# Two adapter layers with Strassen-like weight products: s3 and t3 ahead of t1, an earlier half of a21, b21 copied at once, batch 0's sums on VectorE

## The reference

```python
def _L0_cond_ref(x, labeler_index, W, lora_A, lora_B_w):        # lora_A: (5, 1024, 32), lora_B_w: (1024, 32)
    base = jnp.einsum('bsi,oi->bso', x, W)
    low = jnp.einsum('bsi,bir->bsr', x, lora_A[labeler_index])
    return base + jnp.einsum('bsr,or->bso', low, lora_B_w) * (16 / 32)

def _L1_cond_ref(x, adapter_mapping, W, b, lora_As, lora_Bs):   # lora_As: (32, 1024, 16), lora_Bs: (32, 16, 1024)
    base_out = jnp.einsum('bti,oi->bto', x, W) + b
    lora_h = jnp.einsum('bti,bir->btr', x, lora_As[adapter_mapping])
    return base_out + jnp.einsum('btr,bro->bto', lora_h, lora_Bs[adapter_mapping]) * (32 / 16)

x = x + _L0_cond_ref(x, itok_B_0_2, L0_cond_W, L0_cond_lora_A, L0_cond_lora_B_w)    # x: (8, 256, 1024)
x = x + _L1_cond_ref(x, itok_B_0_23, L1_cond_W, L1_cond_b, L1_cond_lora_As, L1_cond_lora_Bs)
```

## Time and profile before

| what | value |
|---|---|
| median of 3 runs | 321.42 us (320.12 to 324.49) |
| the profiled execution | 322.18 us, of which its span is 320.4 us |
| PE busy | 304.6 us (95%) |
| DVE, ACT, POOL busy | 235.1 us (73%), 140.8 us (44%), 69.1 us (22%) |
| V made, first matmul of batch 0 | 119.21 us |
| first low-rank matmul of batch 0 | 144.60 us |

### The profile page before, as it was taken

The page is one execution under the profiler, slowest core; times in us unless marked ns, Lnnn a source line. Parts: engine busy times, 40 slices in busy tenths (PEclk is TensorE's granted clock), DMA queues, the critical chain, the costliest instruction groups (busy, mean ns, idle before and its releaser), DMA issues.

```text
span 320.4 us, 4335 instructions
## 1 busy us (share of the span) xinstructions
PE 304.6 (95%) x1397; PEld 247.8 (77%) x1397; DVE 235.1 (73%) x310; ACT 140.8 (44%) x223; POOL 69.1 (22%) x84
## 2 busy tenths in 40 slices
PE   7995998999999997789999999999999999999995
PEld 5884887788888886547878878878878878878874
DVE  2539885697999999997687687687677777776321
ACT  4554364939647715333424524425424424335110
POOL 5610000010005500061025034033043052052000
PEclk9999899999999999959999999999999999999999
DMA  6999400430003510046246255255264165103002
GB/s 197 303 356 239 54 0 2 72 61 2 0 0 53 88 25 0 1 67 164 57 77 155 57 91 138 57 85 144 57 101 138 48 101 160 25 8 123 0 33 99
DMA packets 99362, 27.55 MB, mean 86 GB/s; under 512 B 84885, under 2 KB 93077, under 8 KB 99350
## 3 DMA queue, kind: packets, MB, share of 16 engines
q1 hardware_dynamic: 99350, 27.41, 36.9%
HBM read 19.01 MB, written 8.39 MB: 86 GB/s over the span
## 4 chain that ended last, share of the span: by engine, by line
PE 67%; DVE 21%; issue 6%; ACT 3%; DMA 1%; SPq 0%; DVEq 0%
PE bank L980 65%; DVE vt_lo L617 4%; DVE xt L815 2%; PE bank L1002 2%; DVE s_lo L617 2%; DVE vt L617 2%; DVE v L617 1%; DVE t_lo L617 1%; DVE t L617 1%; DMA n<-in_L_cond_W 1%; DVE lhs_lo L617 1%; DVE v_lo L617 1%; DVE s L617 1%; DVE a_lo L617 1%; ACT a_hi L417 1%
## 5 line engine op out<-in xcount | busy, mean ns | idle before, releaser
L980 PE MATMUL bank<-vt_hi,s_hi 128*128 128x512 f32 x96 | 37.5, 390 | 0.0
L980 PE MATMUL bank<-vt_lo,s_hi 128*128 128x512 f32 x96 | 37.5, 390 | 0.0
L980 PE MATMUL bank<-vt_hi,s_lo 128*128 128x512 f32 x96 | 37.4, 389 | 0.0
L815 DVE STREAM_TRANSPOSE xt<-raw 128x512 int32<-128x512 int32 x32 | 32.2, 1081 | 0.0
L417 ACT ACTIVATE lhs_hi<-xt 128x512 fp32r<-128x512 f32 x32 | 19.8, 630 | 28.0 <-PE bank L980 17.8
L617 DVE TENSOR_TENSOR s_lo<-s_sum,s_hi 128x512 fp32r<-128x512 f32 x32 | 27.6, 886 | 2.9 <-ACT s_hi L417 2.9
L980 PE MATMUL bank<-v_hi,lhs_hi 128*128 128x512 f32 x64 | 26.0, 406 | 3.4 <-issue 3.4
L617 DVE TENSOR_TENSOR lhs_lo<-xt,lhs_hi 128x512 fp32r<-128x512 f32 x32 | 24.7, 778 | 4.4 <-ACT lhs_hi L417 4.1
L417 ACT ACTIVATE s_hi<-s_sum 128x512 fp32r<-128x512 f32 x32 | 19.9, 629 | 17.5 <-PE bank L980 9.3
L980 PE MATMUL bank<-v_lo,lhs_hi 128*128 128x512 f32 x64 | 26.8, 419 | 0.0
L980 PE MATMUL bank<-v_hi,lhs_lo 128*128 128x512 f32 x64 | 25.8, 403 | 0.0
(11 more groups left out here) (163 smaller groups left out, 754.4 us busy)
## 6 DMA issues: line engine op xcount, KB each, us to landing
raw<-in_x SPq DMA_DIRECT2D x32, 256.0 KB, 4.9
out<-y SPq DMA_DIRECT2D x32, 256.0 KB, 2.1
n<-in_L_cond_W SPq DMA_DIRECT2D x16, 256.0 KB, 5.2
a<-in_L_cond_W SPq DMA_DIRECT2D x16, 256.0 KB, 5.3
a_raw<-in_L_cond_lora_A SPq DMA_DIRECT2D x8, 128.0 KB, 2.4
a_raw<-in_L_cond_lora_As SPq DMA_DIRECT2D x8, 64.0 KB, 2.4
b_raw<-in_L_cond_lora_Bs SPq DMA_DIRECT2D x8, 64.0 KB, 2.0
b_raw<-in_L_cond_lora_B_w SPq DMA_DIRECT2D x1, 128.0 KB, 5.7
```

Source lines behind the costliest of these rows:

```text
L815: nc.vector.transpose(xt[:, n, :, :].rearrange("p e (s sb) -> p sb e s", sb=GR).bitcast(I32), rows[:, n // 2, n % 2].bitcast(I32)).then_in ...
L980: return nc.tensor.matmul(ps, lhsT, rhs, start=start, stop=stop, skip_group_check=more)
```

## The change

It moves work between places and engines and adds none but a few waits. On SP two of a21's four loads go ahead of n12's. On PE the turns of b22 and b12 stand earlier between M1's last rows of matmuls, the last b12 turn ahead of `q_step`, and the last b21 turn inside M6's second half. On DVE s3 and t3 are made first and t1 after them, `t1_t3` is split in two, and many sums and low parts of the V stage stand in another order (s1's low parts ahead of s4's, t4's low parts before M3's results are added). The two semaphore offsets S1_AT and S4_AT change places with them. ACT copies each row of b21 to `b21` right behind its high part, and PE then waits for the low part instead of the copy before it turns into that bank; ACT's `ym` copies, t1 and v11 high parts move too. Batch 0's four sums go from POOL (`sums(0)`) to DVE (`first_sum`), and in batch 0 `u_total` stands ahead of all four turns of the next x. The loop body of batches 1 to 7 has the same instructions in the same order.

```diff
@@ sync
+            for j in range(0, 2):
+                load_a(a21, 1, 0, j, a21_in[0])
             for j in range(HK):
                 load_n(n12, 1, 0, j, n12_in[j // 2])
-            for j in range(HK):
-                load_a(a21, 1, 0, j, a21_in[j // 2])
+            for j in range(2, HK):
+                load_a(a21, 1, 0, j, a21_in[1])
@@ gpsimd
-            pool.wait_ge(v_done, M3 + HK)
-            sums(0)
             pool.wait_ge(c_lo_made, 2)
@@ scalar
-            for m in range(HK):
-                act.wait_ge(v_done, M1 + m + 1)
-                bank_copy(m1, m, LOW[m], vm1_made)
-            for h in range(2):
-                act.wait_ge(t3_made, 2 * h + 2)
-                high(t3_hi, t3, PAIR[h], t_hi_made)
-                act.wait_ge(s3_made, h + 1)
-                high(s3_hi, s3, PAIR[h], vs_hi_made)
+            m1_copies(range(2))
+            s3_high(0)
+            t3_high(0)
+            m1_copies(range(2, HK))
+            s3_high(1)
+            t3_high(1)
...
                 bank_copy(b21_hi, j, TURN_BANK[j % 3], w1_hi_made)
-                act.wait_ge(w1_lo_made, HK + j + 1)
                 bank_copy(b21, j, TURN_BANK[j % 3], w1_made)
@@ vector
-            t1_t3(0)
-            t1_t3(1)
             s3_sum(0)
-            t1_t3(2)
+            t3_sum(0)
+            t3_sum(1)
+            t1_sum(0)
+            t1_sum(1)
+            s3_low(0)
             t3_low(0)
-            s3_low(0)
-            t1_t3(3)
             s3_sum(1)
+            t3_sum(2)
+            t3_sum(3)
+            s3_low(1)
             t3_low(1)
-            s3_low(1)
             for h in range(2):
+                if h == 1:
+                    t1_sum(2)
+                    t1_sum(3)
+                t2_sum(h)
                 s1_sum(h)
                 s2_sum(h)
-                t2_sum(h)
                 t2_low(h)
                 s2_low(h)
...
-            vt23(0)
-            vt23(1)
-            for h in range(2):
-                dve.wait_ge(t_hi_made, T4_AT + h + 1)
-                low(t4_lo, t4, t4_hi, PAIR[h], t_lo_made)
-            vt23(2)
             dve.wait_ge(q_done, 2)
-            turn_x(0, range(1))
-            vt23(3)
-            turn_x(0, range(1, 4))
+            for m in range(HK):
+                vt23(m)
+                turn_x(0, (m,))
             for m in range(HK):
                 vt23_low(m)
+            dve.wait_ge(xt_made, 4)
+            first_sum(0, xt[:, 2, :, :], xt[:, 3, :, :], ALU.add)
+            dve.wait_ge(s_sum_made, 1)
+            first_sum(1, s_sum[:, 0, :, :], xt[:, 0, :, :], ALU.subtract)
+            first_sum(2, xt[:, 0, :, :], xt[:, 2, :, :], ALU.subtract)
+            dve.wait_ge(s_sum_made, 2)
+            first_sum(3, xt[:, 1, :, :], s_sum[:, 1, :, :], ALU.subtract)
...
                 tt(u2_sum[:, :], BANK_B[:, :], m1_sum[:, :], ALU.add, u2_made)
+                if first:
+                    dve.wait_ge(zeroed, 4)
+                    u_total(b)
                 if not final:
                     dve.wait_ge(s_sum_made, 4 * b + 4)
                     turn_next(b + 1, range(2))
-                if first:
-                    dve.wait_ge(zeroed, 4)
-                else:
+                if not first:
                     dve.wait_ge(u_lo_made, b)
-                u_total(b)
+                    u_total(b)
@@ tensor
                 elif 2 * HK <= old < 3 * HK:
-                    pe.wait_ge(t3_made, old - 2 * HK + 1)
+                    pe.wait_ge(t1_made, old - 2 * HK + 1)
                 elif old >= 3 * HK:
-                    pe.wait_ge(w1_made, old - HK + 1)
+                    pe.wait_ge(w1_lo_made, old - 2 * HK + 1)
...
-            turn_b21(HK - 1)
-            pe.wait_ge(w1_lo_made, 2 * HK)
             for j in range(HK):
+                pe.wait_ge(w1_lo_made, HK + j + 1)
                 last = q_step(Q_BANK[0], HK + j, B21, j, False, j == HK - 1)
```

More of the change, by code:

```diff
@@ L442, in _, with m1_copies, s3_high, t3_high @@
                 bank_copy(b22, j, TURN_BANK[(HK + j) % 3], w1_made)
-            for m in range(HK):
-                act.wait_ge(v_done, M1 + m + 1)
-                bank_copy(m1, m, LOW[m], vm1_made)
-            for h in range(2):
+            def m1_copies(rows):
+                for m in rows:
+                    act.wait_ge(v_done, M1 + m + 1)
+                    bank_copy(m1, m, LOW[m], vm1_made)
+            def s3_high(h):
+                act.wait_ge(s3_made, h + 1)
+                high(s3_hi, s3, PAIR[h], vs_hi_made)
+            def t3_high(h):
                 act.wait_ge(t3_made, 2 * h + 2)
                 high(t3_hi, t3, PAIR[h], t_hi_made)
-                act.wait_ge(s3_made, h + 1)
-                high(s3_hi, s3, PAIR[h], vs_hi_made)
+            m1_copies(range(2))
[4 more added lines that the diff above has]
+            t3_high(1)
             def s2_t2_high(h):
@@ L474, in _ @@
                 high(a12_hi, a12, j, w0_hi_made)
-            for m in range(HK):
-                bank_copy(ym, m, LOW[m], vy_made)
             def q_half(h):
@@ L495, in _ @@
             copy(ct[:, 0:H], C_BANK[0][:, :], ct_made)
+            for h in range(2):
+                high(s1_hi, s1, PAIR[h], vs_hi_made)
             act.wait_ge(b0a1_done, 1)
             copy(q_part[:, 0:G1], B0A1_BANK[64:96, 0:G1], b0a1_part_made, LORA0_SCALE)
-            act.wait_ge(b0a1_all_made, 1)
-            q_half(1)
-            p_high(1)
             act.wait_ge(vs_lo_made, S2_AT + 2)
@@ L504, in _ @@
                 high(s4_hi, s4, PAIR[h], vs_hi_made)
-            for h in range(2):
-                high(s1_hi, s1, PAIR[h], vs_hi_made)
+            act.wait_ge(b0a1_all_made, 1)
+            q_half(1)
+            p_high(1)
+            for m in range(HK):
+                bank_copy(ym, m, LOW[m], vy_made)
             for h in range(2):
@@ L509, in _, with v11_high @@
                 high(a22_hi, a22, PAIR[h], w0_hi_made)
-            for m in range(HK):
+            def v11_high(m):
                 act.wait_ge(v11_made, m + 1)
@@ L514, in _ @@
                 high(t1_hi, t1, PAIR[h], t_hi_made)
+            for m in range(HK - 1):
+                v11_high(m)
             act.wait_ge(t_lo_made, T2_AT + 2)
@@ L760, in _, with b21_low @@
             tt(a1d[:, :, :], raw_a1[:, HK:KT, :], raw_a1[:, 0:HK, :], ALU.subtract, a1d_made)
-            for j in range(HK):
-                dve.wait_ge(w1_hi_made, HK + j + 1)
+            def b21_low(j):
+                dve.wait_ge(w1_made, 2 * HK + j + 1)
                 tt(b21_lo[:, j, :], TURN_BANK[j % 3][:, :], b21_hi[:, j, :].bitcast(F32), ALU.subtract, w1_lo_made)
+            b21_low(0)
+            b21_low(1)
+            t4_sum(0)
+            b21_low(2)
+            b21_low(3)
             for j in range(HK):
@@ L769, in _ @@
             b22_low(1)
+            s4_sum(0)
+            s4_sum(1)
+            p_low(0)
             dve.wait_ge(a1d_made, 1)
@@ L782, in _ @@
                                            in1=q_part[:, 0:G1], op0=ALU.mult, op1=ALU.add).then_inc(b0a1_all_made, 1)
+            s1_low(0)
+            s1_low(1)
             q_half(1)
[L784 removed]
             for h in range(2):
@@ L787, in _, with t1_low, t4_low @@
                 low(s4_lo, s4, s4_hi, PAIR[h], vs_lo_made)
+            p_low(1)
+            def t1_low(h):
+                dve.wait_ge(t_hi_made, T1_AT + h + 1)
+                low(t1_lo, t1, t1_hi, PAIR[h], t_lo_made)
+            def t4_low(h):
+                dve.wait_ge(t_hi_made, T4_AT + h + 1)
+                low(t4_lo, t4, t4_hi, PAIR[h], t_lo_made)
             def v11_sum(m):
@@ L795, in _ @@
             v11_sum(0)
+            a22_low(0)
+            a22_low(1)
             v11_sum(1)
-            s1_low(0)
             v11_sum(2)
-            s1_low(1)
+            t1_low(0)
+            t1_low(1)
             v11_sum(3)
-            for h in range(2):
-                a22_low(h)
+            t4_low(0)
+            t4_low(1)
             for m in range(HK):
                 v11_low(m)
-            for h in range(2):
-                dve.wait_ge(t_hi_made, T1_AT + h + 1)
-                low(t1_lo, t1, t1_hi, PAIR[h], t_lo_made)
             def turn_x(b, quarters):
@@ L880, in h_and_low @@
                 tt(u_st[64:64 + UB, :], u_sum[0:UB, :], u_st[0:UB, :].bitcast(F32), ALU.subtract, u_lo_made)
-            a0_low(0)
             for g in range(4):
                 a_low(0, g)
+            for h in range(2):
+                dve.wait_ge(c_hi_made, h + 1)
+                tt(c_lo[:, HK * h:HK * h + HK, :], CT_BANK[h][:, :].rearrange("p (t n) -> p t n", t=HK),
+                   c_hi[:, HK * h:HK * h + HK, :].bitcast(F32), ALU.subtract, c_lo_made)
+            a0_low(0)
             for j in range(4):
@@ L1107, in _ @@
                     by_halves(h, S2, T2, m, v_done)
+                    if h == 1 and m == 2:
+                        turn_b21(HK - 1)
                 if h == 0:
```

36 lines of the change are left out of this document (17 added, 19 removed).

## The result

The changed kernel took 310.52 us (median of 4 runs, 309.16 to 311.65) against 321.7 us (4 runs, 320.12 to 324.49): ratio 0.964, 95% interval 0.956 to 0.973. Its profiled execution took 311.65 us, with a span of 309.8. The prediction had 310.0 for the median and 308.8 for the span (310.6 - 1.8).

What follows compares the result with a forecast made beforehand. Limits in turn: DVE's low parts for M7, then PE, then DVE's backlog, met in batch 0. `low_rank` -13.2, clock +1.6, total -11.6: the profiled execution's 322.18 becomes 310.6, median 310.0; range 307.5 to 315.5.

Steps and rivals of the forecast that it cites:

- M7: In the front: M7 starts at 26.2, 3.4 us earlier, without a pause, so the clock stays full, 1.6 us more.
- b21's `q_step`: Behind M6: starts at 49.75 instead of 56.53, 6.8 us in all, of which 1.6 is the pause ahead of it.
- The margin of 0.4: Ahead of M6's second half: DVE's low parts done at 43.4, needed at 43.8, so no stall.
- DVE's backlog: From a22's low part (68.4) to the end of U's split in batch 0: 69.75 shrinks to 62.7, ending at 131.4.
- contention: In vt2's and vt3's splits: POOL's sums stretch four of eight to 1.77 from 0.68; moving the sums saves 4.4 us.
- The earlier U is what makes this the only pause: Batch 0: U leaves its bank at 122.3, so the product before `low_rank` starts at once and PE waits only at `low_rank`.
- the pause of 3.35: In batch 0 before the change: PE's idle time before 137.40, counted as lost and expected to go.
- The pause and the clock: At `low_rank` in batch 0: PE waits 2.8 us, and the low clock behind it costs 1.6, ends 0 and 3.6.
- Rival 4: Clock stays low behind batch 0's pause, into the loop: 45 us at half clock would be 331; chance 0.03.
- Rival 2: DVE does not start on a22 6.4 earlier, its backlog absorbs the front: gain about 4 to 5, 316.5; chance 0.08.
- rival 3: The splits' 1.77 came from x's load under way, not POOL's sums, and remains: +4.4, 314.2; chance 0.04.
- Rival 1: The front stays late: a miss opens a pause ahead of M7 or in M6, price 3.4 + 1.6, 315.0; chance 0.10.

Runs made afterwards that it cites:

- experiment 8: The changed kernel without the V stage's new order on DVE and ACT and without the earlier U: 314.65 us, ratio 0.978.
- experiment 1: The changed kernel with batch 0's four sums back on POOL: 314.81 us, ratio 0.980.
- experiment 2: The changed kernel with `u_total` behind two transposes again, as before the change: 309.78 us, ratio 0.967.
- experiment 9: The changed kernel with only the V stage's order as before, the earlier U kept: 316.4 us, ratio 0.984.
- experiment 5: The changed kernel with all of a21 loaded behind n12 again: 311.19 us, ratio 0.967.
- experiment 3: The kernel before with the change's front alone (load order, s3 and t3 first, PE's turns, b21's copies): 315.37 us, ratio 0.984.
- experiment 4: The kernel before with batch 0's four sums on DVE as the only change: 320.36 us, ratio 0.997.

## Why the prediction was right, and where not

**M7** was forecast at 26.2 and came at 27.14. PE was free at 26.75 instead of 26.2, mostly because M1 began at 8.04 instead of 7.31: the second turn of n11 waited 1.3 us for its load, where it had waited 0.6. The other 0.39 (the row calls 0.23 of it idle) was for t3's low part, which ended at 27.04, at a length of 1.49 instead of the 1.21 of the earlier trace rows, while POOL added the eye to a22 beside it. The prediction had left 0.15 between the two. The clock stayed at full speed behind M7, 1.6 us, as forecast.

**b21's `q_step`** came at 51.18, not 49.75, so the front gave 5.35 us and not 6.8. M7's lateness is 0.94 of the 1.43. The margin of 0.4 ahead of M6's second half is the next: s2's low part ended at 43.85 + 1.23 = 45.08, and M6's second half started at 45.13, behind a wait of 0.28 of PE's weight load. From M7 to there are 17.99 us instead of 17.6, and from there to `q_step` 6.05 instead of 5.95. The pause ahead of `q_step` is gone, as forecast.

**DVE's backlog** was the best part. Forecast 63.0 from a22's low part to the end of U's split (68.4 to 131.4), measured 62.55. The front was 1.45 late at a22 (69.85 for 68.4), and the backlog gave 0.45 of that back. Its three terms stood apart in the runs: low parts moved into earlier pauses -5.15 (experiment 8: 4.2 moved, 4.7 less in the last stretch), contention -4.4 (the eight splits 9.29 before and 4.85 now; experiment 1: 3.3 + 1.1), sums +2.5 (2.55). The worth of the move was underrated: 4.4 - 2.5 is 1.9, and experiment 1 showed 3.4. Of the 1.5 between them 1.06 is the op that writes `ac`: in the change it is done before POOL's next sums begin (127.49 against 127.93), in experiment 1 it runs into the first of them.

**"The earlier U is what makes this the only pause"** is the step that failed. Undone in the change it costs nothing (experiment 2), and without the V stage's order it only moves the wait to low_rank (experiment 9). What removed the pause of 3.35 is that DVE reaches U earlier, and for that the order of the V stage is worth 4.7 us from M7 to the split (110.0 against 105.3) and 3.7 to 4.1 of time (314.65 against 310.98 and 310.52). The order does this with U early (105.3 in the change) or late (105.3 in experiment 2), and the early U gained nothing with either order. Which part of the order does it, DVE's or ACT's, was not tried apart.

**The pause and the clock.** 2.8 us forecast, 2.25 measured. U's split ended 1.0 later than forecast, but PE also got to low_rank later, at 130.21 instead of 128.6: 1.36 of that is batch 0's late start, and the rest is PE's own work, 16.45 for 16.2. The 3.0 taken for the stretch from the product with corr to low_rank was too little: it takes 3.63 at full clock (126.58 to 130.21), so that of the "up to 3.6" lost there before the change 3.0 were the clock's. In the profiled execution 8 matmuls at 0.427 instead of 0.227 cost 1.6, as forecast; that the clock does not fall in every execution was not foreseen.

**The load of a21**: s3's sum, which waits for it, started at 17.87, so it landed later than the 16.5 forecast and cost nothing, as said; that it also brings nothing (experiment 5) the prediction did not say.

**The sum.** Batch 0 started 1.36 later than forecast (113.76 for 112.4), low_rank 1.06 (132.46 for 131.4), and from there to the end it took 177.34 where the forecast had 177.4. So the profiled execution is 1.05 above its forecast of 310.6, and the front's lateness is the cause. That the median is within 0.5 of its forecast is in part luck: this execution is the longest of its four, and the ten of the same kernel lie between 309.16 and 311.77, since the clock falls behind the pause in some and not in others, which the prediction did not have. Rival 4's 331 does not follow from its own rate: 45 us at half clock cost 21, which gives about 330.

Rival 2 (backlog absorbs the front) fell by experiment 3, rival 3 (another cause for 1.77) by experiment 1, rival 4 by the loop's windows. Rival 1's miss at a margin was real, for 0.28 us in M6. The change alone does not settle rival 3, since its share of DMA from 90 to 95 us is 0.06. Experiments 1 and 4 do: sums without a load stretch the split, and a load without sums does not.

Not tried: b21's copies, or s3 and t3 ahead of t1, without the rest of the front.

## What to carry to other kernels

Before moving an elementwise op to an idle engine, look in the trace at how long its neighbour's ops last beside it: here four sums on POOL cost DVE 4.4 us, more than the 2.5 of making them itself. When several edits shorten one engine's backlog, price them together by where the backlog starts and ends, since the same edit was worth 1.1 to 1.9 us alone and 4.3 or more with the others, and an edit of the order where the bank was not waited for was worth nothing. For the last pause, list what PE needs from the late engine (here `z_sum` and the split of U) and put all of it, not the first item alone, ahead of work for the next batch.
